# Far values and row maxima added by one packed pass of four 32-row matmuls at the head of each period

## The reference

```python
def block(x):                                   # x: (2, 2048, 256)
    h = layernorm(x)
    q, k, v = heads(h @ wq), heads(h @ wk), heads(h @ wv)      # 16 heads of 64
    scores = einsum('bhqd,bhkd->bhqk', q, k) + rel_bias[bucket(k_pos - q_pos)]
    out = einsum('bhqk,bhkd->bhqd', softmax(scores), v) @ wo
    x = x + layernorm(out)
    gates = softmax over the two best of 8 experts, from the mean token
    ffn = sum_e gates_e * gelu(layernorm(x) @ expert_w[e].T + expert_b[e])
    return x + layernorm(ffn)
```

## Time and profile before

| | us |
|---|---|
| median of 3 runs | 2945.34 |
| the profiled execution | 2945.1 |
| its span | 2943.3 |
| PE busy | 2811.5 (96%) |
| POOL busy | 2414.9 (82%) |
| DVE busy | 1769.3 (60%) |
| ACT busy | 1663.7 (57%) |

### The profile page before, as it was taken

One profiled execution on the slowest core, in us unless ns is written; L12 is line 12 of the kernel. 1 busy time (PEld: TensorE's weight loads), 2 busy tenths in 40 slices (PEclk: granted clock), 3 DMA queues, 4 the chain that ended last, 5 costly groups with the idle time before them and its releaser, 6 DMA issues.

```text
span 2943.3 us, 49274 instructions
## 1 busy us (share of the span) xinstructions
PE 2811.5 (96%) x18720; PEld 1043.8 (35%) x18720; DVE 1769.3 (60%) x4532; ACT 1663.7 (57%) x2117; POOL 2414.9 (82%) x1098
## 2 busy tenths in 40 slices
PE   5999999999999999999999999999999999977897
PEld 2333333333333333333333333333333333322443
DVE  7556555565655556655655566655656565584666
ACT  4555565555555555555555555556555655556576
POOL 0789999999989998999989899999999898988000
PEclk9999999999999999999999999999999999999999
DMA  5000000000000000000000000000000000101001
GB/s 159 26 5 9 9 26 9 5 8 13 21 9 5 9 26 9 9 5 26 9 9 9 5 26 9 8 9 23 8 9 8 9 12 9 65 8 33 4 1 58
DMA packets 48256, 52.69 MB, mean 18 GB/s; under 512 B 16482, under 2 KB 38114, under 8 KB 48018
## 3 DMA queue, kind: packets, MB, share of 16 engines
q1 hardware_dynamic: 48018, 49.52, 5.6%
HBM read 44.57 MB, written 10.82 MB: 19 GB/s over the span
## 4 chain that ended last, share of the span: by engine, by line
PE 58%; issue 18%; DVE 17%; POOL 4%; ACT 3%; DMA 0%; SPq 0%; DVEq 0%; ACTq 0%; POOLq 0%
PE po L635 20%; PE st L605 19%; PE pre L617 6%; PE pm L572 4%; POOL acc L540 4%; PE st L860 3%; DVE mpart L1311 3%; DVE pre L1303 2%; DVE st L1328 2%; PE pm L578 2%; DVE pre L1308 2%; PE pm L659 2%; PE pm L644 1%; DVE y L1350 1%; DVE mpart L1303 1%
## 5 line engine op out<-in xcount | busy, mean ns | idle before, releaser
L540 POOL TENSOR_TENSOR acc<-acc,prob 128x1024 f32<-128x1024 f32 x896 | 2115.2, 2361 | 222.4 <-ACT prob L948 133.9
L948 ACT ACTIVATE prob<-st 128x1024 f32<-128x1024 f32 x1024 | 1016.0, 1021 | 902.3 <-DVE st L1328 823.5
L635 PE MATMUL po<-prob,v 128*64 128x512 f32 x4096 | 994.5, 606 | 0.0
L605 PE MATMUL st<-qk 64*128 64x512 f16 x6144 | 835.0, 378 | 6.9 <-ACT prob L948 4.9
L1303 DVE CUSTOM_DVE_ANT_0 pre<-pre,ew 128x512 f32<-128x512 f32 x448 | 300.6, 712 | 562.0 <-issue 561.9
L1308 DVE CUSTOM_DVE_ANT_0 pre<-pre,tab 128x512 f32<-128x512 f32 x704 | 475.2, 715 | 150.8 <-issue 150.7
L605 PEld LDWEIGHTS st<-qk 64*128 64x128 f16 x6144 | 294.1, 94 | 329.6 <-ACT prob L948 43.3
L635 PEld LDWEIGHTS po<-prob,v 128*64 128x64 f32 x4096 | 249.0, 136 | 447.5 <-issue 374.0
L605 PE MATMUL st<-eq,ek 64*128 64x512 f16 x2048 | 390.0, 377 | 0.0
L617 PE MATMUL pre<-qk 64*128 64x512 f16 x1600 | 310.1, 384 | 42.1 <-ACT ew L978 18.9
L1311 DVE TENSOR_REDUCE mpart<-pre 128x2 f32<-128x1024 f32 x224 | 271.4, 1211 | 115.7 <-PE pre L617 114.9
(11 more groups left out here) (199 smaller groups left out, 2369.3 us busy)
## 6 DMA issues: line engine op xcount, KB each, us to landing
inv_b<-inv_scratch SPq DMA_DIRECT2D x130, 128.0 KB, 2.9
t_scratch<-w_scratch SPq DMA_DIRECT2D x2, 2688.0 KB
qk<-x SPq DMA_DIRECT2D x8, 512.0 KB, 5.5
out<-qk SPq DMA_DIRECT2D x8, 512.0 KB, 3.5
w<-w_pairs SPq DMA_DIRECT2D x8, 384.0 KB, 3.7
t2f<-t_scratch SPq DMA_DIRECT2D x8, 384.0 KB, 4.6
t<-t_scratch SPq DMA_DIRECT2D x8, 384.0 KB, 3.3
den_c<-den_s SPq DMA_DIRECT2D x130, 2.0 KB, 1.7
```

The lines of the kernel that those rows point to most:

```text
L540: nc.gpsimd.tensor_tensor(acc[g % 2][:, :, :], a, prob[:, n % RING, :, :], ALU.add).then_inc(sum_p, 1)
L605: last = nc.tensor.matmul(st[:, 2 * (n % 2) + h, :], w[64 * h:64 * h + 64, :], t[64 * h:64 * h + 64, :], start=(r == 0), stop=(r == len(te ...
L635: last = nc.tensor.matmul(po[64 * h:64 * h + 64, :], v[:, g // CHUNKS, j, 64 * h:64 * h + 64], prob[:, n % RING, h, :], start=(s == 0), st ...
L948: nc.scalar.activation(prob[:, n % RING, :, :], st[:, 2 * (n % 2):2 * (n % 2) + 2, :], ACT.Exp).then_inc(exp_done, 1)
```

## The change

**One pass.** The `ek` by `eq` product leaves `scores`. A new function `score_rows` does it for both steps of a period at once: four matmuls, each on 32 rows of the array (rows 0, 32, 64, 96 and on), one per head and step, into the four banks of `st`, as the first write of each bank. It stands at the head of the period, ahead of piece n, and takes over the waits of both steps. To have the operands in four places, `M_ROW` moves from 32 to 8, the constant rows repeat every 32 partitions, `max_in` sends four DMAs per chunk instead of two, and `far_rows` writes four parts of 8 partitions instead of two of 32 (it runs twice per pair of heads).

**Pieces.** `piece_plan` orders the pieces after the less/pair ones anew: at odd numbers (first places of a period) "single" while there are any, at even numbers "near".

**Bands.** `BAND_STEPS` moves two bands, from steps 8 and 10 to 7 and 11, so that all are on odd steps; on DVE both bands of a period come ahead of the second piece's maximum.

```diff
-BAND_STEPS = [3, 5, 8, 10, 13, 15]
+BAND_STEPS = [3, 5, 7, 11, 13, 15]
-M_ROW = 32
+M_ROW = 2 * QT
...
-    return rest[:1] + pairs + rest[1:]
+    first = 1 + len(pairs)
+    single, near = [[piece for piece in rest[1:] if piece[2] == way] for way in ("single", "near")]
+    order = []
+    for u in range(first, PIECES):
+        kinds = (single, near) if u % 2 else (near, single)
+        order.append((kinds[0] or kinds[1]).pop(0))
+    return rest[:1] + pairs + order
...
-                for h in range(2):
-                    sp.dma_start(eq[64 * h + M_ROW:64 * h + M_ROW + 1, g % 2, :].rearrange("p (t q) -> p t q", q=128),
+                for k in range(4):
+                    h = k % 2
+                    sp.dma_start(eq[32 * k + M_ROW:32 * k + M_ROW + 1, g % 2, :].rearrange("p (t q) -> p t q", q=128),
                                  mrow[QT * h:QT * h + QT, :]).then_inc(m_in, 16)
...
-                         (kl[b][:, keys], qh[b][:, queries]), (ek[:, variant(c, j), :], eq[:, g % 2, :])]
+                         (kl[b][:, keys], qh[b][:, queries])]
...
-                                                start=(r == 0), stop=(r == len(terms) - 1))
+                                                start=False, stop=(r == len(terms) - 1))
                 last.then_inc(st_ready, 1)
+            def score_rows(i, n):
+                g = step_of(n)[0]
+                for d in range(2):
+                    scores_wait(i, n + d)
+                for d in range(2):
+                    j = step_of(n + d)[2]
+                    for h in range(2):
+                        k = 2 * d + h
+                        nc.tensor.matmul(st[:, k, :], ek[32 * k:32 * k + 32, variant(g % CHUNKS, j), :],
+                                         eq[32 * k:32 * k + 32, g % 2, :], start=True, stop=False)
...
                 for n in range(0, STEPS, 2):
+                    if not last or n + 2 < STEPS:
+                        score_rows(i, n + 2)
                     next_piece(n)
                     for m in (n + 2, n + 3):
                         if not last or m < STEPS:
-                            scores_wait(i, m)
                             scores(m)
                     next_piece(n + 1)
...
                     if not last or n + 2 < STEPS:
                         bands = band(i, n + 2, bands)
-                    next_maximum(n + 1)
                     if not last or n + 3 < STEPS:
                         bands = band(i, n + 3, bands)
+                    next_maximum(n + 1)
```

More of the change, by code:

```diff
@@ L179, in shape_tables @@
     rows = np.zeros((128, ROWS), np.float32)
-    r = np.arange(128) % 64
+    r = np.arange(128) % 32
     for t in range(QT):
@@ L587, in scores_wait @@
                 if s == 0:
-                    pe.wait_ge(m_in, (G + 1) * 32)
+                    pe.wait_ge(m_in, (G + 1) * 64)
                     if g < 2:
-                        pe.wait_ge(far_set, (i + n // STEPS) * 4 + 2 * g + 2)
+                        pe.wait_ge(far_set, (i + n // STEPS) * 8 + 4 * g + 4)
                     if c == 0:
@@ L739, in _ @@
             pe.wait_ge(xl_v, B * KT * GROUPS)
+            score_rows(0, 0)
             for n in range(2):
-                scores_wait(0, n)
                 scores(n)
@@ L951, in far_rows @@
             def far_rows(pair, buf):
[L953 to L956, removed]
+                for k in range(4):
+                    part = slice(32 * k, 32 * k + 2 * QT)
+                    nc.scalar.activation(eq[part, buf, :].rearrange("p (t q) -> p t q", q=128),
+                                         rowc[part, 0:QT].unsqueeze(2).broadcast_to((2 * QT, QT, 128)), ACT.Copy,
+                                         scale=farv[part, 0, bass.ds(2 * pair + k % 2, 1)]).then_inc(far_set, 1)
             def next_table(i, part):
@@ L1260, in far_rows @@
             def far_rows(pair, buf):
[L1263 to L1266, removed]
+                for k in range(4):
+                    part = slice(32 * k, 32 * k + 2 * QT)
+                    nc.vector.tensor_scalar(eq[part, buf, :].rearrange("p (t q) -> p t q", q=128),
+                                            rowc[part, 0:QT].unsqueeze(2).broadcast_to((2 * QT, QT, 128)),
+                                            farv[part, 0, bass.ds(2 * pair + k % 2, 1)], None, ALU.mult).then_inc(far_set, 1)
             def pair_table(pair, k):
```

## The result

| | before | after |
|---|---|---|
| median of 4 runs, us | 2944.84 | 2961.28 |
| lowest to highest, us | 2944.24 to 2945.95 | 2960.14 to 2962.03 |
| the profiled execution, us (span) | 2945.1 (2943.3) | 2961.76 (2960.0) |
| PE busy, us | 2811.5 | 2789.7 |
| ACT busy, us | 1663.7 | 1726.4 |

The ratio is 1.0055, 95% interval 1.004 to 1.007. I forecast 2921 us. PE is busy 22 us less and the kernel takes 16 us more, so PE's idle time has grown by some 38 us: more than the work removed from PE has come back as idle time.

What follows compares the result with a forecast made beforehand. PE's order bounds the kernel, hiding release chains of 1.55 to 1.90 us. +1.99 - 3.54 = -1.55 us per four chunks, -23 over 15 cycles, about 1 more in the last: 2945.1 - 24 = 2921, range 2902 to 2976.

Steps and rivals of the forecast that it cites:

- The release chain of a piece: Between a period's two pieces: the next waits until the first is read, 1.79 us (single), 1.90 (near), 1.55 (less).
- The pass: At the period's head, ahead of the first piece: four matmuls at 0.217 us plus a 0.09 change of shape, together 0.31.
- the net of the periods: Second piece against 1.95 us: less 0.09 earlier, single 0.15 later, near 0.26 later; sum +1.99 us per four chunks.
- The waits that the moved bands take away: Periods lengthened by late exponentials behind bands on DVE: 3.74 us per four chunks, of which 3.54 taken as gained.
- My check of the exponential at the head: The odd step's exponential ends at 4.07 us, before the next head's pass is due at 4.28: hidden by 0.2.
- the rest at nothing: Extra `max_in` DMAs and `far_rows` operations on ACT are covered and cost nothing; uncovered, up to 30 and 22 us.
- E: Rival: the change doesn't move the time, as gains and losses of 1.99 and 3.54 nearly cancel: 2945 us; 7 in 100.
- A: Rival: PE alone counts, piece reads are no limit; each period gains 0.12 and the waits go: 2831 us; 6 in 100.
- B: Rival: the pass takes a third more than one pair's 0.217, each period grows by 0.07: 2957 us; 12 in 100.
- D: Rival: the pass runs as two, each period 0.22 longer than forecast: 3032 us; 5 in 100.
- C: Rival: the pass waits at the head for an exponential formerly asked for 1.09 us later; 53 us return: 2974; 12 in 100.
- the two signs by which I would have called myself wrong: PE's pass waiting for ACT `prob` at the heads in more than a few periods, or periods without jobs at 4.0 us.

Runs made afterwards that it cites:

- e6: e1 with the single reduction of a piece in first place reading only 256 of 512 columns of each head: 2901.4 us.
- e10: e1 with the projection job of periods 2, 4 and 6 moved ahead of the second piece on PE: 2925.9 us.
- e5: e1 with the pass of four matmuls issued twice at the head of each period: 3048.9 us.
- e1: The changed kernel with its four far-value operations split, two behind the projection's copy (step 5) and two in step 9: 2945.7 us.
- e3: The kernel before with only the bands moved (odd steps, ahead of the second piece's maximum): 2919.0 us.
- e4: The kernel before with only the pass of four matmuls and its layout, old piece order and old bands: 3161.9 us.
- e2: The kernel before with the new piece order and the moved bands, without the pass: 2926.9 us.
- e8: e3 with the band of step 11 moved to step 9 and the two far-value operations behind the projection's copy: 2909.1 us.

## Why the prediction was wrong

**What bounds the kernel: right.** The release chain of a piece (1.79, 1.90, 1.55) was read from the trace of before and came out at 1.79, 1.89 and 1.57. That the time of the work removed between the pieces comes back as idle time is shown by e6 and e10.

**The pass: 0.31 forecast, 0.33 measured.** Its four streams run at the rate of one pair (e5); the change of shape from 32 to 64 rows costs 0.11 and not the 0.09 of the changes before. The Trainium skill's 3.07 times (TensorE: Matmul & The Clock Gate, Measured speedup vs the span model), by which one pass would take an estimated 0.28 us without the change of shape, is not borne out in this stream: 0.22 (e5).

**First failed step: the net of the periods, mis-sized.** It stood at +1.99 us per four chunks and came out at 3.15. In the periods of pairs two to seven, "single" cost 0.17 (I had 0.15), "near" 0.28 (0.26) and once 0.37, "less" gained 0.04 (0.09). Each miss is 0.02 to 0.05, but there are 64 periods per pair: 2.3 us per pair. I gave the sum of +1.99 and -3.54 a margin of 0.05 on 18 periods, and none on the 14 "less" periods, of whose small gain more than half was gone.

**The waits that the moved bands take away: right in kind, nearly in size.** In e1 the pairs gain 0.52 us each; with the costs above (26 x 0.17 + 10 x 0.28 + 0.2 - 28 x 0.04 = 6.3) that makes 6.8 of waits gone, where I had 7.1. My check of the exponential at the head held everywhere but in a few periods: PE waited for it 0.7 us between 1100 and 2000.

**Second failed step: the rest at nothing.** I put `far_rows` at nothing because it runs in periods of which ACT uses half; if uncovered, it was to cost 1.4 x 16 = 22 us. It was uncovered: 15.6 us (e1). The mistake is in the reason that I gave. A free half of ACT's time covers nothing if the operation stands ahead of one that others wait for. Behind these four stand, on ACT, the copy of the projection, behind that on DVE its lower half, and behind that the reduction that releases the piece. The row of DVE's lower half ahead of the reduction in the earlier trace rows already showed this chain, and the trace of before has the two far-value operations in it, between the exponentials and the next copy:

```profile
1078.64 1.94 ACT L948 ACTIVATE prob<-st 128x1024 f32<-128x1024 f32 x2 [0.65 <-PE st L605]
...
1080.47 1.44 ACT L954 ACTIVATE eq<-rowc,farv 32x512 f16<-32x512 f32 x2
...
1081.94 0.60 ACT L929 ACTIVATE qk<-pm 128x512 f16<-128x512 f32 x1
```

There the chain still ended in time: in this pair period 6 is 5.53, as in the second chunk. My sentence that with the moved bands none of the old causes of waiting remains fails at the same place: in e3, with the two operations of before, the band at step 7 already makes this period 6.12.

**The sum of it.** Forecast 2921, measured 2961: 40 us. Of these 15.6 are the far values (e1 against after). The pairs one to seven have 2.6 each, 18, from the sizes above (2.3) and the waits (0.3). The rest, some 6, is in the last pair, where e1 loses 3.3 us and I had counted a gain of 2.5. So the mis-sized net and the far values weigh about alike: without the far values the forecast gain of 24 was gone already (e1), and with them the kernel is slower. In the last pair the pieces run out, periods are 4 to 15 us long, and DVE and ACT do the first layer norms. Nearly all of e1's loss there, 3.1 us, lies between the start of its seventh chunk and the end of the program. This stretch takes 321.9 us in before and 322.4 in e4, which has the pass and the old bands; with the moved bands it takes 324.2 in e3 and e2, without the pass, and 325.0 in e1. So some 2.3 of the 3.1 come with the moved bands and not with the pass. Which wait brings this about no run isolates; it stays open.

**The rivals.** E came true of the change without its far-value cost (e1). A is refuted by e6, B and D by e5. The measured 2961 lies between the numbers of B (2957) and C (2974), but by accident: neither mechanism acts in after. C, the wait at the head, is not what made it slower (two waits, 0.7 us, between 1100 and 2000), but e4 shows that its mechanism exists and how large it is when the bands stay. Of the two signs by which I would have called myself wrong, waits at the heads and periods of 4.0, neither showed: none of them looks at what stands behind an added operation on ACT.

## What to carry to other kernels

Before work is taken out from between two uses of the same buffer, the distance that the buffer's own release wants is to be held against the work that is left: here 1.79 to 1.90 us against 1.52, so of 0.43 us removed only 0.06 behind a near piece and 0.17 behind a single one shortened that stretch (0.38 behind a "less" piece, 1.57). Where an operation is added, ask what stands behind it in its engine's order, not how busy the engine is. And when a change has several parts, run them apart: here the part that looked like an accessory (the bands) held all of the gain, 0.9% alone and 1.2% when set with care, and the part that gave the change its name cost 19 us on top of the other two with the far values moved out of the way (e1 against e2), and 34 where the change has them (after against e2).

## What the runs showed of the hardware

At a granted clock of 1.00, four matmuls of 32 rows and 512 columns, on four row groups and into four banks, took 0.22 us together, as long as two of 64 rows (e5). A change from 32-row to 64-row matmuls took 0.11 us (0.33 from the pass to the piece, less 0.22). From 64 rows by 128 columns to 128 rows by 64 columns it took 0.09 (0.31 from the piece to the values in the earlier trace rows, less 0.22), and back 0.10 (1.87 from the values to the next piece, against 1.77 from values to denominators, which have the same shape). An ACT operation on 8 partitions by 512 elements took 0.71 (median of 60 in after; four in a row 2.93), no less than one on 32 partitions in before (0.71, median of 30; two in a row 1.44): splitting the work by partitions doubled its time. One DVE operation (L1338, 128x256) took 0.41 us in e8 where it started ahead of POOL's addition, and 2.33 to 2.42 where it started 0.21 to 0.30 behind the start of one.
